# Rearranging the opening of a two-layer gated cross-attention and mixture-of-experts kernel: context first, mask and bias split later, tokens transposed between key products

## What is computed

```python
x = x + tanh(g_xattn[0]) * xattn0(layernorm(x), ctx, ctx, mask)   # logits + mask * -1e9
x = x + tanh(g_ffn[0])   * experts0(layernorm(x))                 # silu(x Wg) * (x Wu) Wd
x = x + tanh(g_xattn[1]) * xattn1(layernorm(x), ctx, ctx)
x = x + tanh(g_ffn[1])   * experts1(layernorm(x))                 # relu(x W1)^2 W2

# xattn: q = x Wq + bq; k = ctx Wk + bk; v = ctx Wv + bv
#        softmax(q k^T / 4 [+ mask]) v Wo + bo
```

## Time and profile before

| | us |
|---|---|
| median of 3 runs | 757.09 (756.56 to 759.33) |
| the profiled execution | 756.57 |
| its span, first to last instruction | 754.8 |
| PE busy | 684.7 (91%) |
| DVE busy | 414.9 (55%) |
| ACT busy | 273.9 (36%) |
| POOL busy | 213.0 (28%) |

### The profile page before, as it was taken

How to read it: one execution, slowest core, us unless ns; L and a number is a source line. 1 busy time by engine, 2 the same in 40 slices (tenths; PEclk the granted TensorE clock), 3 DMA queues, 4 the chain that set the end, 5 groups by cost and what they waited for, 6 DMA issues and landing times.

```text
span 754.8 us, 17644 instructions
## 1 busy us (share of the span) xinstructions
PE 684.7 (91%) x5904; PEld 517.5 (69%) x5904; DVE 414.9 (55%) x1385; ACT 273.9 (36%) x528; POOL 213.0 (28%) x399
## 2 busy tenths in 40 slices
PE   5798999989999999999999999979888898999970
PEld 3676777647777777777777777666666665778850
DVE  4677888853334333233233233369998987554426
ACT  2566566522112112112112112246655552445530
POOL 4122554471111111111111111112244556444440
PEclk9999999999999999999999999999999999999995
DMA  9033564461141131111101100241022232644429
GB/s 225 14 118 126 189 204 159 148 226 50 50 119 36 37 81 35 36 29 36 36 29 36 35 29 15 68 177 30 30 74 71 65 107 73 172 125 120 123 82 334
DMA packets 50857, 70.72 MB, mean 94 GB/s; under 512 B 7687, under 2 KB 38023, under 8 KB 50771
## 3 DMA queue, kind: packets, MB, share of 16 engines
q1 hardware_dynamic: 42380, 50.85, 22.5%
q0 software_dynamic: 6816, 18.69, 7.0%
q10 hardware_dynamic: 1575, 0.05, 0.2%
HBM read 46.55 MB, written 23.02 MB: 92 GB/s over the span
## 4 chain that ended last, share of the span: by engine, by line
PE 72%; DVE 16%; issue 5%; DMA 3%; POOL 2%; ACT 2%; DVEq 0%; POOLq 0%; SPq 0%; ACTq 0%
PE ps L1499 28%; PE ps L1529 17%; PE ps L1299 4%; PE ps L1512 3%; DVE m_rows L841 3%; DVE x_sb L825 3%; PE ps L1237 2%; PE ps L1312 2%; PE ps L1485 2%; PE ps L1265 2%; PE ps L1291 2%; PE ps L1254 2%; DVE ctx_q L858 2%; PE ps L1215 1%; DVE x_sb L875 1%
## 5 line engine op out<-in xcount | busy, mean ns | idle before, releaser
L1499 PE MATMUL ps<-w_all,share 128*128 x780 | 227.6, 439 | 2.7 <-DVE share L1118 2.7
L1499 PEld LDWEIGHTS ps<-w_all,share 128*128 128x128 f32 x780 | 144.2, 190 | 63.4 <-issue 5.2
L551 POOL DMA_INDIRECT ys_dram<-share,dest_i x78 | 75.4, 967 | 327.3 <-DVE share L1129 277.1
L1529 PE MATMUL ps<-w_all,share 112*128 (+1 forms) x624 | 148.0, 380 | 1.7 <-ACT share L737 1.0
L1529 PEld LDWEIGHTS ps<-w_all,share 112*128 112x128 f32 (+1 forms) x624 | 112.4, 190 | 15.1 <-issue 2.6
L1145 DVE TENSOR_TENSOR share<-share,ps 128x344 f32<-128x344 f32 x78 | 40.1, 514 | 138.6 <-PE ps L1499 77.4
L726 ACT COPY share<-ps 128x512 f32<-128x512 f32 x39 | 22.9, 586 | 152.0 <-PE ps L1512 152.0
L841 DVE TENSOR_REDUCE m_rows<-ps 128x8 f32<-128x960 f32 x64 | 70.4, 1139 | 11.2 <-PE ps L1254 11.1
L723 ACT ACTIVATE share<-ps 128x344 f32<-128x344 f32 x78 | 35.7, 458 | 104.5 <-PE ps L1499 104.5
L544 POOL DMA_INDIRECT xs_dram<-xn,slot_now x64 | 63.6, 994 | 21.4 <-issue 14.6
L514 POOL TENSOR_SCALAR nm<-mv 128x1 f32<-128x1 f32 (+1 forms) x48 | 12.1, 253 | 158.0 <-DVE mv L881 110.9
(11 more groups left out here) (204 smaller groups left out, 1005.0 us busy)
## 6 DMA issues: line engine op xcount, KB each, us to landing
share<-xs_dram SPq DMA_DIRECT2D x78, 129.0 KB, 2.1
w_all<-ys_dram SPq DMA_DIRECT2D x16, 512.0 KB, 7.0
w_all<-gate SPq DMA_DIRECT2D x8, 688.0 KB
w_all<-up SPq DMA_DIRECT2D x8, 688.0 KB
w_all<-down SPq DMA_DIRECT2D x8, 560.0 KB
w_all<-w SPq DMA_DIRECT2D x16, 256.0 KB
xs_dram<-q_flat SPq DMA_DIRECT2D x17, 129.0 KB, 2.6
out<-x_sb SPq DMA_DIRECT2D x8, 256.0 KB, 5.3
```

The costliest lines, as they stand in the source:

```text
L551: g.indirect_dma_start(ys_dram, bass.IndirectOffsetOnAxis(ap=dest_i[:, u:u + 1], axis=0), y_sb[:, u, :], None).then_inc(D_y[u], 16)
L1499: i = t.matmul(ps[:, bank, 0:w], xgT[:, k, :], w_all[:, bass.ds(off + (k * UPW[l] + col - EW[l]), w)], start=(k == 0), stop=(k == KT - 1))
L1529: i = t.matmul(ps[:, 6, 0:D], hT[0:r, c + KD[1] * (j % 2) * l, :], w_all[0:r, bass.ds(off + (KT * UPW[l] + c * D - EW[l]), D)], start=(c = ...
```

## The change

- SP: the context of sequences 0 to 3 is issued ahead of the tokens of sequence 0.
- ACT: a one-column activation on `ident` (`first_act`) stands behind the small loads and brings the table load with it. `ctx_evac(0)` now stands ahead of `ln1_apply(B0)`, `xnT_evac` between the two `k_evac`, `q_evac` and the layer norm of sequence 1 ahead of the tanh.
- PE: 6 products of the identity with itself (128x256, results never read) stand ahead of `ctx_t(0)`, 2 behind it. `x_t(B0)` stands between the two `k_proj`. The waits for wo and for the split bias stand ahead of the first `out_proj` and no longer ahead of the first unit.
- DVE: `split_mask` works in three pieces. Piece 0 (sequences 0 and 1, 128x240) stays in the opening, piece 1 (sequences 2 and 3, 128x240) comes in unit 1 and piece 2 (sequences 4 to 7, 128x480) in unit 3, both ahead of `divide`. PE waits for them ahead of the scores that need them (u = 3 and 7). `split_bias(0)` comes in unit 0 ahead of `divide`, the scaling of the mask columns behind the first `split_max`.
- `mask_f` and `mask_hi` lie in the part of `w_all` that expert 5 gets later, since `share` is in use by then.

```diff
-        mask_f = share[:, 0:NB * K].rearrange("p (b k) -> p b k", b=NB)
+        mask_at = (NE - 3) * EW[0]
+        mask_f = w_all[:, mask_at:mask_at + NB * K].rearrange("p (b k) -> p b k", b=NB)
...
+            load_ctx(0)
             sp.dma_start(x_sb[:, 0:2, :], xv[:, 0:2, :]).then_inc(L_x[0], 16)
-            load_ctx(0)
             load_att(0, 1, L_wk)
...
+            a.wait_ge(C_id, 2)
+            a.activation(first_act[:, :], ident[:, 0:1], ACT.Identity, scale=ident[:, 0:1])
...
                 if l == 0:
+                    ctx_evac(0)
                     ln1_apply(B0)
-                    ctx_evac(0)
                     k_evac(0, 0)
+                    xnT_evac(B0, 2)
                     k_evac(0, 1)
-                    xnT_evac(B0, 2)
+                    q_evac(B0, (3, 1))
+                    ln1_apply(B0 + 1)
                     a.wait_ge(L_gates, 48)
                     a.activation(tg[:, :], gates[:, :], ACT.Tanh).then_inc(C_a, 1)
-                    q_evac(B0, (3, 1))
-                    ln1_apply(B0 + 1)
...
-            def split_mask():
+            def split_mask(piece):
+                a, z = ((0, 2), (2, 4), (4, NB))[piece]
+                part_f, part_hi, at_ = mask_f[:, a:z, :], mask_hi[:, a:z, :], 6 * piece
...
-                    split_mask()
-                    v.wait_ge(L_mcol, 16)
-                    v.tensor_scalar(mask_col[0:K, :], mask_col[0:K, :], NEG, None, ALU.mult).then_inc(C_v, 2)
+                    split_mask(0)
                     ln1_stats(B0 + 1)
                     values(B0, 6)
-                    v.wait_ge(C_a, 1)
-                    split_bias(0)
...
+                    if l == 0 and u == 0:
+                        v.wait_ge(C_a, 1)
+                        split_bias(0)
+                    if l == 0 and u in (1, 3):
+                        split_mask(1 + u // 2)
                     divide(G)
...
+                    def first_products(n):
+                        for _ in range(n):
+                            t.matmul(ps[:, 7, 0:2 * P].rearrange("p (j n) -> p j n", j=2), ident[:, :],
+                                     ident[:, :].unsqueeze(1).to_broadcast([P, 2, P]), start=True, stop=True)
+
+                    first_products(6)
                     ctx_t(0)
+                    first_products(2)
                     t.wait_ge(L_wk, 16)
                     k_proj(0, 0)
+                    x_t(B0, 2)
                     k_proj(0, 1)
-                    x_t(B0, 2)
...
-                t.wait_ge(L_wo, 32 * (l + 1))
-                t.wait_ge(C_bo, l + 1)
                 t.wait_ge(*((L_vr, 32) if l == 0 else (L_small1, 48)))
...
+                        if l == 0 and u in (3, 7):
+                            t.wait_ge(d_m, 6 * (2 + u // 7))
                         scores(G + 1)
...
+                    if u == 1:
+                        t.wait_ge(L_wo, 32 * (l + 1))
+                        t.wait_ge(C_bo, l + 1)
                     if u >= 1:
                         out_proj(G - 1)
```

More of the change, by code:

```diff
@@ L135, in flamingo_kernel @@
         yg = w_all[:, NE * EW[1]:NE * EW[1] + NB * QT * TOPK * D].rearrange("p (b t k d) -> p b t k d", b=NB, t=QT, k=TOPK)
-        mask_f = share[:, 0:NB * K].rearrange("p (b k) -> p b k", b=NB)
-        mask_hi = share[:, NB * K:NB * K + NB * K // 2].bitcast(BF16).rearrange("p (b k) -> p b k", b=NB)
+        mask_at = (NE - 3) * EW[0]
+        mask_f = w_all[:, mask_at:mask_at + NB * K].rearrange("p (b k) -> p b k", b=NB)
+        mask_hi = w_all[:, mask_at + NB * K:mask_at + NB * K + NB * K // 2].bitcast(BF16).rearrange("p (b k) -> p b k", b=NB)
         ctx_q = sb("ctx_q", [P, 2 * (2 * P + DH)])
@@ L195, in flamingo_kernel @@
         ident = sb("ident", [P, P])
+        first_act = sb("first_act", [P, 1])
         hmask = sb("hmask", [P, HP])
@@ L774, in query_bias @@
                                 qs[:, :].unsqueeze(1).to_broadcast([P, KT, 2]), ALU.mult).then_inc(C_q, 1)
-            def split_mask():
[L779 to L782, removed]
+            def split_mask(piece):
+                a, z = ((0, 2), (2, 4), (4, NB))[piece]
+                part_f, part_hi, at_ = mask_f[:, a:z, :], mask_hi[:, a:z, :], 6 * piece
+                if piece == 0:
+                    v.wait_ge(L_mask, 64)
+                    v.wait_ge(C_e, 3)
+                v.tensor_scalar(part_f, part_f, mk[:, 0:1], -NEG, ALU.mult, ALU.mult).then_inc(d_m, 1)
+                v.wait_ge(d_m, at_ + 1)
                 for part in range(1, 3):
-                    v.tensor_copy(mask_hi, mask_f).then_inc(d_m, 1)
-                    v.wait_ge(d_m, 2 * part)
-                    v.scalar_tensor_tensor(out=mask_f, in0=mask_hi, scalar=mk[:, 1:2] if part == 1 else sel[:, 2:3], in1=mask_f,
+                    v.tensor_copy(part_hi, part_f).then_inc(d_m, 1)
+                    v.wait_ge(d_m, at_ + 2 * part)
+                    v.scalar_tensor_tensor(out=part_f, in0=part_hi, scalar=mk[:, 1:2] if part == 1 else sel[:, 2:3], in1=part_f,
                                            op0=ALU.mult, op1=ALU.add).then_inc(d_m, 1)
-                    v.wait_ge(d_m, 2 * part + 1)
-                v.tensor_copy(mask3[:, :, :], mask_f).then_inc(d_m, 1)
+                    v.wait_ge(d_m, at_ + 2 * part + 1)
+                v.tensor_copy(mask3[:, a:z, :], part_f).then_inc(d_m, 1)
             def split_bias(l):
@@ L961, in _ @@
                 if l == 0:
+                    v.wait_ge(L_mcol, 16)
+                    v.tensor_scalar(mask_col[0:K, :], mask_col[0:K, :], NEG, None, ALU.mult).then_inc(C_v, 2)
                     values(B0 + 1, 4)
```

## The result

The changed kernel takes 753.48 us (median of 20 runs, 750.36 to 755.85), the kernel before 757.41 us on the same occasion (20 runs, 754.79 to 760.17). The ratio is **0.9945, 95% interval 0.9932 to 0.9958**: faster by 0.55%, 3.2 to 5.2 us. The forecast was 752.8 us and 0.57%.

The account below looks back on a forecast made before the run. PE bounds the kernel (busy 684.7 of 754.8 us), leaving 70 us without products and slow products at 1.2 GHz to win. 756.57 - 5.8 + 1.3 + 0.2 = 752.3, plus 0.5 for the median: 752.8 us, range 750.8 to 756.5.

Parts of the forecast that it names:

- Opening, 5.8 us: From the first instruction to the first row maxima: these start at 17.3 instead of 23.09 us, a gain of 5.8 us.
- The path: Opening: token landing, layer norm and transposes, not the key products, set the time; transposes at 10.5, done with keys by 12.6.
- Unit 0, nothing: Unit 0: the bias split (2.3 us) fits in DVE's wait for PE's weighted values, so nothing is counted.
- Unit 1, 1.3 us: Unit 1: mask piece 1 (2.2 us) delays DVE, so `out_proj` waits for row maxima; cost 1.3 us, between nothing and 2.2.
- Unit 3, 0.2 us: Unit 3: mask piece 2 (3.2 us) mostly fits DVE's idle 2.77 us; cost 0.2 us, between nothing and 3.2.
- The tanh, nothing: ACT: the later tanh costs nothing, as what it waits for landed or ran earlier than needed.
- Rival 1: Opening: the clock stays at 1.2 GHz through the key products; 3.5 us of gain gone, 756.3 us; chance 0.10.
- The weak form: Opening: only the context transposes are slow; keys at 9.0 to 10.6, moving the token path by 0.1.
- Rivals 2, 3 and 5: Tokens land late, 754.3 (0.15); DVE's pieces cost little, 751.3 (0.15); change doesn't do what it says, near 757 (0.01).
- Rival 4: Unit 1: PE's new wait drops the clock; units 1 and 2 at 1.2 GHz cost 14 us, 766.8; chance 0.04.
- A reading: Opening of the kernel before: token transposes at 16.13 take less than half as much each as the slow context transposes.
- The sum: Whole kernel: 756.57 - 5.8 + 1.3 + 0.2 = 752.3 us, forecast as 752.8 us, 0.57% faster.

Follow-up runs that it names:

- e1: The changed kernel without the 8 products of the identity; ratio to the kernel before 0.9962 (0.9924 to 1.0001).
- e3: The changed kernel with the tokens of sequence 0 loaded first again, the context second; ratio to the kernel before 0.9966 (0.9926 to 1.0005).
- e7: The kernel before with only the 6 and 2 products of the identity added; ratio to the kernel before 0.9967 (0.9926 to 1.0008).
- e10: The changed kernel with two mask pieces (none in unit 1) and tokens loaded first, repeated on a third chip; 788.05 us, ratio to the kernel before 0.9956.
- e4: The changed kernel with mask piece 1 behind the bias of the values in unit 1, not ahead of the division; ratio to the kernel before 0.9929.
- e5: The changed kernel with the tanh of the gates back ahead of the query copies on ACT; ratio to the kernel before 0.9984 (0.9959 to 1.0009).
- e8: The changed kernel with the output bias split back in the opening, behind the first bias of the values; ratio to the kernel before 0.9958.
- e12: The changed kernel without the early activation that brings the table load; ratio to the kernel before 0.9974 (0.9943 to 1.0005).
- e9: The changed kernel itself, timed again on a third chip; 788.79 us, ratio to the kernel before 0.9923 (0.9885 to 0.9961).
- e6: The changed kernel with two mask pieces (none in unit 1) and tokens loaded first; 750.65 us from four executions, ratio to the kernel before 0.9903.

## Why the prediction was right, point by point

- **Opening, 5.8 us.** Measured 5.92 at the first maxima and 5.91 at `max_t`. Single starts were foretold within 0.4 us: transposes 6.5 (6.60), keys 8.1 (8.44), tokens 10.5 (10.42), queries 12.6 (12.53), scores 16.0 (15.84), maxima 17.3 (17.17). The context lands later than the estimate of 5.1 (5.62 in e1), under the same cover. The six products took 5.16 us (4.95 estimated).
- **The path.** "This path, not the keys, sets the time" was too strong: the two are nearly level, as e3 shows.
- **Unit 0, nothing.** The bias split cost nothing. Something was gained there, which the prediction put at nothing: from the copy of the maxima to the next scores 0.09 us instead of 0.30, and at the shifted scores of unit 1 the lead is 36.29 - 30.16 = 6.13 us. The moved wait for wo and the bias is the likely cause: e7, which doesn't have it moved, still takes 0.30 us there, e10 0.09.
- **Unit 1, 1.3 us.** Measured 6.13 - 4.65 = 1.48. Size and cause (DVE's work behind the piece comes late) were right, the place was wrong. The step that failed: "PE needs `divide(1)`'s first step for the product at 43.05; that is ready at 42.3 + 0.7, just in time". The product also waits for the bias of the values, the last step ahead of the maxima, 1.5 us later. e4 shows both waits, one in the place of the other.
- **Unit 3, 0.2 us.** Measured nothing: the maxima of unit 4 are 4.65 us ahead, as the shifted scores of unit 2 were. The 0.2 us came from taking for `divide(3)` the time of unit 1 (2.2 us), which has the bias of the values in it; without it, it took 56.62 - 54.66 = 1.96. (The prediction's own starts, 59.4 and 2.2, give 0.3 and not 0.2.)
- **The tanh, nothing.** True of the move, but its price if it had stayed was not worked out: 4.15 us at unit 4 (e5).
- **Rival 1** (the clock stays low) did not happen in any profile with the products: a key half took 1.7 to 1.9 us in each. What it leaned on, that 4.9 us of products are less than the 5.9 us of work ahead of the rise before, did not matter: the clock rose within the first six products or just behind them. The weak form happened in part: transposes took 0.98 to 1.32 us.
- **Rivals 2, 3 and 5** did not happen. The tokens landed at 6.54 (6.96 at the latest, in e4), not at 8.0; piece 1 cost 1.48 us and not nothing; and the context copy waited for the transposes alone.
- **Rival 4** (the clock falls in unit 1) exists, smaller than priced: in e8 and e12, two of the eight profiles that have the wait of 1.7 us at that place, for 1.7 us each. The six profiles without the wait don't have the fall. The changed kernel's and e9's profiles don't show it; whether other executions of the changed kernel have it is open.
- **A reading.** The transposes of the tokens at 16.13 take 0.15 us each, those of the context at 6.50 0.23: two thirds, not "less than half". That PE ran slowly until about 16 rests on the key products, and holds.

The sum (4.3 us) met the measured 3.2 to 5.2 us and the mark's 4.65 us. The mechanism was right in the opening, which carries the gain. That the time came within 0.7 us is in part luck: at the mark the errors add up to 0.35 us too little gain (0.12 in the opening, 0.21 in unit 0, 0.2 in unit 3, less 0.18 in unit 1), and nothing was allowed for what goes behind it, such as the 1.0 us at the first expert block.

## What to carry to other kernels

Where an engine waits for a load at the start, throw-away products bring the clock up before the real ones. They are nearly free if they end when the load lands: here the transposes began up to 1.3 us after the context was there (6.88 in e9, 5.62 in e1), and the later landing of wk left 0.3 us of that at the keys (8.83, 8.52). So measure their worth at the first step behind the opening.

When work is pushed behind an engine's step, list every wait of the partner on anything behind it, and not just on the next result.

A wait that costs nothing today (the tanh for a bias) sets the time once the work around it moves forward, so each such wait needs its landing time beside it.

## What was new about the hardware

- In all fourteen profiles the record of the granted clock reads 1.00 from the start to 16 us. In the kernel before it does so over 10 to 12 us while products take twice their time.
- A gap of 1.7 us on PE was followed by half clock in two profiles and by full clock in six, at the same place of nearly the same program; what decides is not shown. It costs 1.7 us (10.83 against 9.15 us between two marks). In the attention of layer 1 the same fall stands once in the profile of before and twice in that of the changed kernel; falls of this size fit the scatter of 5 us between executions, but only the profiled ones have a record.
- Six products of the identity took 4.42 to 5.49 us, and in one and the same kernel 5.47 (e6) and 4.42 us (e10): the moment at which the clock rises differs between executions.
